# A vision tower with two attentions, a routed feed-forward and an adapter attention: the first attention regrouped into one pipeline, maxima subtracted in PSUM, and more filling matmuls

## The reference

```
h = patches(x) @ conv_w + conv_b + pos                         # (32, 25, 192)

# block 0: linear attention, 8 heads of 24, 2 query groups, per image
k = kv[0] * SCALE; v = kv[1]; q = h @ Wq                       # q: 2 groups of 24
attn = softmax(einsum('bghnd,bghne->bghde', k, v), axis=-1)    # 24 x 24 per head
out = einsum('bghde,bgne->bghnd', attn, q);  h = LN(h + out @ Wproj + bproj)

# block 1: 8 experts 192 -> 768 -> 192 with relu, the 2 best of a softmax gate
h = LN(h + sum of gate * expert(h) over the two best)

# block 2: differential attention, 12 heads of 16, two score sets, per image (25 x 25)
out = softmax(q1 k1' / 4) v - exp(lambda) * softmax(q2 k2' / 4) v
h = LN(h + out @ Wo + bo)

# block 3: qkv with an 8-expert low-rank adapter (top 2), then 12 heads of 16
qkv = h @ Wqkv' + bqkv + 2 * delta;  out = softmax(q k' / 4) v
h = LN(h + out @ Wproj' + bproj)
```

## Time and profile before

| | |
|---|---|
| time, median of 3 runs | 361.54 us (361.49 to 362.68) |
| profiled execution | 360.7 us, its span 358.9 us |
| TensorE busy | 320.6 us (89%), mean granted clock 0.935 |
| VectorE, ScalarE, GpSimd busy | 163.5, 88.3 and 70.8 us |
| first attention, to the first gate copy | 26.5 to 82.7 us |
| expert blocks | 98.5 to 200 us |
| second attention's steps, third's | 236.5 to 278.7 us, 315.2 to 351.9 us |

### The profile page before, as it was taken

The page is one execution under the profiler, slowest core; times in us unless marked ns, Lnnn a source line. Parts: engine busy times, 40 slices in busy tenths (PEclk is TensorE's granted clock), DMA queues, the critical chain, the costliest instruction groups (busy, mean ns, idle before and its releaser), DMA issues.

```text
span 358.9 us, 7355 instructions
## 1 busy us (share of the span) xinstructions
PE 320.6 (89%) x3092; PEld 262.5 (73%) x3092; DVE 163.5 (46%) x459; ACT 88.3 (25%) x204; POOL 70.8 (20%) x82
## 2 busy tenths in 40 slices
PE   5999857997799989999999999888999889889992
PEld 4875446885489989999999879754677758446771
DVE  0021357466611111111111077779987552766555
ACT  1021214423012221122111003742332121723230
POOL 8000000056223374433332231000001100000002
PEclk9999955598989999999999899998999999989996
DMA  7999200020016988999991220000000000000002
GB/s 281 336 290 299 67 4 3 2 69 2 11 44 194 299 293 247 285 287 304 303 296 58 79 80 2 0 2 2 5 2 0 3 0 2 0 2 3 2 0 69
DMA packets 11930, 37.91 MB, mean 106 GB/s; under 512 B 1783, under 2 KB 5751, under 8 KB 11666
## 3 DMA queue, kind: packets, MB, share of 16 engines
q1 hardware_dynamic: 9978, 33.52, 29.6%
q0 software_dynamic: 1920, 3.93, 3.6%
HBM read 34.25 MB, written 3.19 MB: 104 GB/s over the span
## 4 chain that ended last, share of the span: by engine, by line
PE 72%; DVE 17%; DMA 3%; issue 3%; ACT 3%; POOL 2%; POOLq 0%; DVEq 0%
PE ps L717 10%; PE ps L705 7%; PE ps L706 7%; PE ps L503 7%; PE ps L533 5%; PE ps L796 4%; PE ps L757 3%; PE ps L749 3%; PE ps L590 2%; PE ps L774 2%; DMA xs<-x_rows,from_row 2%; PE ps L550 2%; PE ps L784 2%; PE ps L577 2%; PE ps L551 2%
## 5 line engine op out<-in xcount | busy, mean ns | idle before, releaser
L435 POOL TENSOR_TENSOR rstd<-veps,neg_half 128x2 f32<-128x2 f32 (+1 forms) x16 | 10.6, 660 | 209.6 <-DVE veps L1151 209.6
L705 PE MATMUL ps<-xga,w1t 128*128 128x128 f32 x240 | 47.4, 279 | 0.0
L706 PE MATMUL ps<-xgb,w1u 65*128 65x128 f32 x240 | 47.4, 279 | 0.0
L1256 DVE COPY ys<-ps 128x192 f32<-128x192 f32 x20 | 7.2, 358 | 77.4 <-PE ps L717 77.4
L717 PE MATMUL ps<-w1t,hid 128*128 128x192 f32 x240 | 42.2, 326 | 0.0
L503 PE MATMUL ps<-w1a,consts 128*128 128x384 f32 x96 | 39.2, 540 | 0.0
L717 PEld LDWEIGHTS ps<-w1t,hid 128*128 128x128 f32 x240 | 38.6, 190 | 0.0
L982 ACT ACTIVATE hid<-ps 128x768 f32<-128x768 f32 x20 | 16.2, 810 | 87.2 <-PE ps L706 87.2
L705 PEld LDWEIGHTS ps<-xga,w1t 128*128 128x128 f32 x240 | 37.3, 195 | 0.1
L706 PEld LDWEIGHTS ps<-xgb,w1u 65*128 65x128 f32 x240 | 37.3, 195 | 0.0
L465 POOL DMA_INDIRECT y_rows<-ys,to_row x20 | 19.8, 988 | 57.4 <-DVE ys L1256 57.1
(11 more groups left out here) (223 smaller groups left out, 538.8 us busy)
## 6 DMA issues: line engine op xcount, KB each, us to landing
w1t<-in_wt SPq DMA_DIRECT2D x20, 960.0 KB, 5.6
w1u<-in_wu SPq DMA_DIRECT2D x20, 240.0 KB, 7.5
pat<-in_pat SPq DMA_DIRECT2D x6, 496.0 KB, 7.0
w1a<-in_w1a SPq DMA_DIRECT2D x1, 1322.0 KB
y<-y_rows SPq DMA_DIRECT2D x6, 192.0 KB, 3.4
w1b<-in_w1b SPq DMA_DIRECT2D x1, 835.2 KB
x_rows<-x_tok SPq DMA_DIRECT2D x3, 192.0 KB, 2.0
out<-x_tok SPq DMA_DIRECT2D x6, 96.0 KB, 1.7
```

The lines of the kernel that those rows point to most:

```text
L705: pe.matmul(out, w1t[:, b, 128 * k:128 * k + 128], xga[:, j % 2, :], start=True, stop=False)
L706: mm = pe.matmul(out, w1u[0:CB + 1, b, 128 * k:128 * k + 128], xgb[:, j % 2, :], start=False, stop=True)
```

## The change: what it does

1. **First attention.** A round now takes four groups and two of their four images (`scores0(r)`, two banks, alternating), so two rounds are in flight. The queries come first, then keys and values of groups 0 to 4, rounds 0 and 1, groups 5 to 7, then rounds 2 and 3. Copies of keys and values are shared out anew between ScalarE and VectorE (which has only groups 1 and 3). The residual is added by TensorE (`residual0`), and the first layer norm reads PSUM.
2. **Later attentions.** VectorE makes only the maxima. TensorE multiplies them by a negative identity matrix into the scores' own banks (`subtract`), and ScalarE exponentiates from there. Scores of group g+2 wait for the exponentials of group g. ScalarE's exponential moves to the end of its step.
3. **Fillers.** In the later attentions they move from ahead of the scores (384 columns, two) to ahead of the transposes, behind the wait for `p1T_done`. New: four of 384 ahead of either attention's steps and ahead of the wait for `y2`; `to_channels` has 384 columns in place of 128; 6 in place of 3 ahead of the ranks, and 7 in place of 4 ahead of the gathered rows.

```diff
@@ to_channels
-                        keep_busy(spare[t // 2], 2)
+                        keep_busy(spare[t // 2], 2, 384)
@@ first attention, TensorE
+            queries()
+            for g in range(5):
+                keys_values(g)
+            keys_by_values(0)
+            keys_by_values(1)
+            for g in range(5, G):
+                keys_values(g)
+            turn_a0(0)
+            keys_by_values(2)
+            keep_busy(4, 6)
+            keys_by_values(3)
+            turn_a0(1)
+            by_queries(0)
+            by_queries(1)
+            pe.wait_ge(s0_shifted, 3)
+            residual0(range(0, 4))
+            turn_a0(2)
+            by_queries(2)
+            turn_a0(3)
+            for t in range(0, 3):
+                project0(t)
+            residual0(range(4, TT))
+            by_queries(3)
+            for t in range(3, TT):
+                project0(t)
+            def residual0(ts):
+                for t in ts:
+                    n = rows(t)
+                    pe.matmul(proj0(t), ident[0:n, 0:n], x_tok[0:n, t, :], start=(t % 2 == 0), stop=False, skip_group_check=True)
@@ routed block
-            keep_busy(3, 3, 384)
+            keep_busy(3, 6, 384)
...
-            keep_busy(3, 4, 384)
+            keep_busy(3, 7, 384)
...
+            keep_busy(4, 4, 384)
             pe.wait_ge(diag_done, PICKS)
@@ attention, TensorE
+                pe.wait_ge(v_act, call + 1)
+                pe.wait_ge(v_dve, call + 1)
+                keep_busy(4, 4, 384)
                 pe.wait_ge(qk_act, QK_JOBS[call])
...
                 def scores(g):
+                    if g >= 2 or call:
+                        pe.wait_ge(s1_exp, G * call + g - 1)
...
+                def subtract(g):
+                    pe.wait_ge(s1_top, G * call + g + 1)
+                    for bank in range(2):
+                        heads = HQ * sum(b == bank for b, *_ in slots)
+                        first = HQ * sum(b < bank for b, *_ in slots)
+                        mm = pe.matmul(ps[:, 2 * (g % 2) + bank, 0:heads * N], neg_ident[:, :], view(st1[:, g % 2, 0, first:first + 1], [[1, heads], [0, N]]),
+                                       start=False, stop=True, skip_group_check=True)
+                    mm.then_inc(s1_sub, 1)
...
                 def turn(g):
                     n = G * call + g
-                    pe.wait_ge(p1_ready, n + 1)
                     if g >= 1:
                         pe.wait_ge(p1T_done, n)
+                    keep_busy(4, 2, 384)
+                    pe.wait_ge(p1_ready, n + 1)
...
                 for step in range(G + 3):
-                    if 2 <= step < G + 2:
-                        pe.wait_ge(s1_shifted, G * call + step - 1)
-                    if 0 < step < G + 2:
-
-                        keep_busy(2 * (step % 2), 2, 384)
+                    if 1 <= step <= G:
+                        subtract(step - 1)
@@ first attention, ScalarE
+            for g in (0, 2, 4):
+                kv_out(g)
+            exp0(0)
+            kv_out(5)
+            exp0(1)
+            kv_out(6)
+            kv_out(7)
+            a0T_out(0)
+            exp0(2)
+            a0T_out(1)
+            exp0(3)
+            a0T_out(2)
             reorder_out(2, 0)
-            a0T_out(2)
+            a0T_out(3)
             reorder_out(3, 0).then_inc(o0_act, 1)
@@ first attention, VectorE
+            kv_out(1)
+            kv_out(3)
+            shift0(0)
+            shift0(1)
+            norm0(0)
+            norm0(1)
+            shift0(2)
+            shift0(3)
+            norm0(2)
+            norm0(3)
@@ attention, VectorE
-                        link(dve.tensor_reduce(top2, src, AX.X, ALU.max))
-                        ins = dve.tensor_tensor(s, src, over(top2, N), ALU.subtract)
-                    ins.then_inc(s1_shifted, 1)
+                        ins = dve.tensor_reduce(top, src, AX.X, ALU.max)
+                    ins.then_inc(s1_top, 1)
```

More of the change, by code:

```diff
@@ L553, in _, with queries @@
-            for n in range(2):
-                out = ps[:, 4 + n, 0:HALF]
-                pe.matmul(out, wq0a, half_of(xpa, n), start=True, stop=False)
-                pe.matmul(out, wq0b, half_of(xpb[0:CB + 1], n), start=False, stop=True).then_inc(q0_ready, 1)
+            def queries():
+                pe.wait_ge(xa_done, 2)
+                pe.wait_ge(xb_done, 2)
+                for n in range(2):
+                    out = ps[:, 6 + n, 0:HALF]
+                    pe.matmul(out, wq0a, half_of(xpa, n), start=True, stop=False)
+                    pe.matmul(out, wq0b, half_of(xpb[0:CB + 1], n), start=False, stop=True).then_inc(q0_ready, 1)
@@ L588, in by_queries @@
                     pe.wait_ge(s0_shifted, 4)
[L589 to L591 removed]
+                for g4 in range(4):
+                    pair = 2 * (4 * (r // 2) + g4) + r % 2
+                    mm = pe.matmul(view(ps[:, O0_BANK[r], 2 * N * g4:2 * N * g4 + 1], [[256, 2], [N, 2], [1, N]]), a0T[:, 4 * r + g4, :],
+                                   q0[:, :, :, pair, :], start=True, stop=True)
@@ L614, in _, with project0 @@
+            def project0(t):
+                half = 1 if 128 * t + rows(t) <= HALF else 2
+                pe.wait_ge(o0_act, half)
+                pe.wait_ge(o0_dve, half)
                 n = rows(t)
                 for s in range(2):
-                    mm = pe.matmul(tok_bank(2, t), view(o0[:, 256 * t + s:256 * t + s + 1], [[2, n]]), wp0[:, s, :], start=(s == 0 and t % 2 == 0), stop=(s == 1), skip_group_check=True)
+                    mm = pe.matmul(proj0(t), view(o0[:, 256 * t + s:256 * t + s + 1], [[2, n]]), wp0[:, s, :], start=False, stop=(s == 1), skip_group_check=True)
@@ L829, in _ @@
             QK_JOBS = [6, 9]
+            pe.wait_ge(neg_done, 1)
             to_channels(2, 4)
@@ L1339, in attention @@
                     if step < G:
-                        shift(step)
+                        top_of(step)
                     if step >= 1:
```

226 lines of the change are left out of this document (99 added, 127 removed).

## The result

The changed kernel takes **379.86 us** (median of four runs, 378.31 to 389.57), the kernel before 361.51 beside it: 1.049 times as long, with a 95% interval of 1.044 to 1.055. The forecast was 365.2 with a range up to 369.6. So the direction was right and the size was not: it lost 18.4 us where 3.7 were expected. The profiled run took 380.68 us, and its span is 378.9. Some executions of a kernel run a few per cent longer at a lower mean clock: medians and spreads here are of all runs, ratios and their intervals of the others alone.

A forecast was written before the change was run, and what follows sets the result against it. TensorE's own work was taken as the bound (72% of the span). Terms -6.7 -1.7 +1.2 +2.4 +1.7 +3.0 +2.3 +1.5 = +3.7 gave 365.2 us on the median; 8-in-10 range 359.6 to 369.6.

The forecast's parts named there:

- First attention: First attention to first layer norm: the new order gains 6.7 us, bounds 2.5 and 8.0.
- I put one such break into rounds 1 and 3.: First attention's rounds: a TensorE break of 0.6 us, seen in the later rounds before, counted in rounds 1 and 3.
- I take it to stay at 2.4 GHz but for that place.: First attention: TensorE's clock stays high except at the longest gap, 3.0 us, during the second reorder.
- Rival B: First attention: clock falls all the same, 369.4 us, or rounds take twice as long, 370.4; chance 0.13.
- Routing: Routing and first expert block: more fillers lie in waits and remove a clock dip; gain 1.7 us, bounds 0 and 1.7.
- Ahead of `y2`: Before the sum of `y2`: four fillers take 2.6 us, faster residual matmuls save part; cost 1.2, bounds 0.6 and 2.6.
- Channels: Channels of the second and third layer norms: wider fillers outlast TensorE's waits; cost 2.4 and 2.3 us, bounds 2.0 and 3.4.
- Ahead of the second attention: Before its first scores: four fillers, 2.6 us, exceed a wait of 0.71; cost 1.7, bounds 1.6 and 1.9.
- Steps of the second attention: Second attention: subtraction on TensorE makes a full step 5.5 us, from 4.50; cost 3.0, bounds 1.0 and 5.2.
- Third attention: Its steps: eight subtractions of 0.5 us added, one filler pair and low clock gone; cost 1.5, bounds 0.5 and 3.
- Rival A: Added fillers are covered by TensorE's waits: 357.6 us, chance 0.10; in part, 360 to 362, chance 0.13.
- Rival C: Later attentions: scores wait for ScalarE's exponentials two groups back, 4.8 us in the second attention: 370 us; chance 0.04.

The follow-up runs named there:

- first_alone: The kernel before with only the new first attention, its banks and its layer norm: 366.6 us (1.016).
- y2_alone: The kernel before with only the four fillers of 384 columns ahead of the sum of `y2`: 364.5 us (1.009).
- fill_alone: The kernel before with only the added or widened fillers outside the attention steps: 372.3 us (1.026).
- first_held: As `first_alone`, with eight more fillers of 384 columns where TensorE waits in the first attention: 362.0 us (0.996 against before).
- sub_bare: As `sub_alone`, without the pair of fillers in each step of both later attentions: 362.8 us (0.998 against before).
- sub_alone: The kernel before with only the subtraction in PSUM and the new place of the step's fillers: 371.7 us (1.030).
- combo_third: `first_alone` plus group 5 between rounds 0 and 1, fillers in waits, two wide ahead of round 3, four ahead of the third attention: 355.3 us (0.984 against before).

## Why the prediction was wrong, step by step

**First attention, the step that failed** (-6.7 forecast, +4.2 in the traces, +5.2 by itself). The single durations were right: five groups in 7.6, rounds in 1.27, reorders in 3.0. Two assumptions under the sum were not. By the forecast's own marks the changed kernel is 0.2 late where the queries start (27.12 for 26.9), 4.3 at the end of round 1 (44.62 for 40.3), 6.6 at the end of round 3 (56.62 for 50.0), 8.8 at the end of the second reorder (74.19 for 65.4) and 11.1 at the second pair's first tile (81.11 for 70.05).

- *"I put one such break into rounds 1 and 3."* The break between rounds 0 and 1 is 2.28 and not 0.65. I had priced it from the rounds of before, which stand apart. Moving work between the rounds gives 4.0 back, in part by the clock behind the break.
- *"I take it to stay at 2.4 GHz but for that place."* The clock was low four times. "That place", the wait during the second reorder, was known to be 3.0 long and nothing was charged for it, though the lower bound of the gain held 4 us for just this. Fillers in the waits give 4.7 back. The queries alone took 5.0 for 2.7, at 0.50; this dip had no wait ahead of it and is not in `first_alone`, so it may belong to this execution alone; only one profile of the changed kernel exists. With both mended the gate comes 5.3 earlier than in before: the term of -6.7 was the value of another kernel, one that nobody had written yet.

Rival B had this mechanism, at 369.4, and 0.13. Its price was of the same kind as the term's lower bound. Both were too small: they counted low clock in the second half of the stage alone and the first break at 0.65, and the later rows lost 5.6 more than forecast besides.

The rule of the Trainium skill weighed there, "TensorEngine Tiling (Array Packing)", Key Properties (tiles of the array run independently of each other), did not bite: a round that reaches two row groups takes 1.27 for 128 records (51.67 above), as one that reached four did.

**Routing** (-1.7; 20.1 to 18.4 in the trace, of which 0.4 goes in the expert blocks). The number came near, and the first expert block ran without a dip, as forecast; that the seven fillers did this is not shown. Kernels without them show the same 18.4, and kernels with them 19.9.

**Ahead of `y2`** (+1.2; +2.7 in the trace, +3.0 by itself). The step "if the residual matmuls run at full speed" held in `y2_alone`, with 1.1, and did not in the changed kernel, where they took 4.33 (4.29 in before), so all of the fillers was paid. Both happen; the size depends on where low clock falls.

**Channels** (+2.4, +2.3; +2.7, +2.6). The wait for the tiles vanished and the fillers' own length was paid, as drawn. `fill_alone` shows the same 2.7 and 2.6.

**Ahead of the second attention** (+1.7; +3.3). `fill_alone`, without a dip ahead of it, has +1.8 for values to first scores, as forecast. The other 1.6 is a dip at 236.4 to 239.8 in the key matmuls (0.51), behind a wait of 1.68 that has no new cause.

**Steps of the second attention** (+3.0; +3.5). Full step 5.55, forecast 5.5, no wait ahead of the transposes:

```profile
271.53 1.17 PE L818 MATMUL ps<-st,neg_ident 128*128 128x300 f32 x4
...
277.08 1.18 PE L818 MATMUL ps<-st,neg_ident 128*128 128x300 f32 x4
```

Two terms were mis-sized. From its start to that of the scores the pair of matmuls of 300 columns takes 1.10 to 1.21, not 1.0, which is 0.8 or more over eight groups; and TensorE's waits were 3.4 and not 4.2 before, so 1.65 of them went and not 2.2.

**Third attention** (+1.5; +2.5). The dip went (35.2 in kernels without one, 36.8 in before); that the fillers did it is not shown. What the steps lost is 4.0 (39.2 against 35.2), forecast 3.1: the subtraction is two matmuls here, of 200 and 100 columns, and takes 0.63 to 0.73 and not 0.5.

**Rival A** (fillers are covered) fell: in both channels stages they were not. **Rival C** (scores wait for exponentials) fell: ScalarE waits for TensorE in the full steps. The Trainium skill, "Perfetto Trace Analysis", Matmul Optimizations, says that the engine scales its power by use and wants matmuls back to back. These runs agree: with fillers in the waits `first_held` is 4.7 shorter, and without the pair in the steps the mean clock of a run of `sub_bare` goes down to 0.87. By the median `sub_bare` is still 8.9 shorter than `sub_alone`, since the pair's own length goes.

## What to carry to other kernels

Price a pipeline that has not run by its durations at both clock levels, and charge the low one behind waits like the 2.1 and 3.1 us here, or fill them. Before moving an operation onto the engine with the least slack, take off the fillers that only kept its clock up: the subtraction lost 10 us with its two fillers and about nothing with one or none. That it gains is not shown, since `combo_third` does as well without it. And test the parts by themselves: here the first attention, a losing part, beat the tuned kernel by 3.5 us once work stood between its rounds and its waits were filled, and by 5.6 in `combo_third`.

## What the runs showed of the hardware

- Short matmuls on tiles of 25 by 32 stop after 206 or 208 records, for 2.1 to 2.3 us, at a fixed place in the stream of instructions, and go on 2.2 to 2.9 us behind a packet of the instruction queue. With 1.5 us of long matmuls in the middle the stop is 0.3 to 0.7.
- The clock of this core is low for a few us at a time, in places that change from kernel to kernel with the same instructions around them (routing 18.4, 20.0 or 21.5 us). What a dip costs depends on whether it falls on fillers ahead of a wait (nothing in `combo_third`) or on work that others wait for (1.6 us). A stage's gain of 1.5 us in one profile proves nothing by itself.
- The steps of the later attentions, busy for 12 of 12 us, held a clock of 1.00, but at their end and behind it the clock was at 0.52 to 0.57 in the three kernels with fewer than one filler a step.
